# Score banks of an attention kernel as one tensor, with joint row maxima and one shift per group

## The reference

```
lat = layer_norm(layernorm(x));  c = layer_norm(ctx)        # with gains and biases
q = lat @ Wq;  k, v = split(concat([c, lat]) @ Wkv)         # 16 heads of 64; 487 keys
dots = q k^T / 8;  attn = softmax(dots);  out = (attn v) @ Wout
x = x + tanh(g_xattn) * out
x = x + tanh(g_ffn) * moe_ffn(layernorm(x))                 # 8 experts, top 2, gelu, width 1024
```

## Time and profile before

| | us |
|---|---|
| median of 3 runs | 1904.99 |
| lowest and highest run | 1902.63, 1905.17 |
| the profiled execution's own time | 1902.62 |
| span of its core in the trace | 1900.9 |
| first and last score maximum (line 495) start at | 74.7 and 1327.4 |
| busy TensorE / VectorE / ScalarE / GpSimd | 1674.2 / 1428.0 / 1195.3 / 1183.0 |

### The profile page before, as it was taken

One profiled execution on the slowest core, in us unless ns is written; L12 is line 12 of the kernel. 1 busy time (PEld: TensorE's weight loads), 2 busy tenths in 40 slices (PEclk: granted clock), 3 DMA queues, 4 the chain that ended last, 5 costly groups with the idle time before them and its releaser, 6 DMA issues. The chain is left out here.

```text
span 1900.9 us, 42714 instructions
## 1 busy us (share of the span) xinstructions
PE 1674.2 (88%) x15031; PEld 1163.1 (61%) x15032; DVE 1428.0 (75%) x2917; ACT 1195.3 (63%) x2666; POOL 1183.0 (62%) x1297
## 2 busy tenths in 40 slices
PE   2899999999999999999999999998402999999980
PEld 1456666666666666666666666665302999989970
DVE  4777888888888888888888888877395666666646
ACT  2587777777777777877777777777254333433320
POOL 4477777777777777777777777767263343333320
PEclk9999999999999999999999999999555999999995
DMA  3267766767767666676776776767455111111119
GB/s 131 46 127 140 142 144 131 139 139 142 147 129 145 138 140 144 135 139 138 139 150 136 136 137 129 138 130 142 118 186 173 46 49 45 50 50 47 47 35 289
DMA packets 599541, 233.18 MB, mean 123 GB/s; under 512 B 534064, under 2 KB 584016, under 8 KB 598992
## 3 DMA queue, kind: packets, MB, share of 16 engines
q1 hardware_dynamic: 592656, 212.67, 52.5%
q0 software_dynamic: 6720, 18.36, 3.1%
HBM read 78.66 MB, written 20.19 MB: 52 GB/s over the span
## 5 line engine op out<-in xcount | busy, mean ns | idle before, releaser
L279 POOL TENSOR_TENSOR p_parts<-p_f,p_parts 112x487 f16<-112x487 f32 x512 | 560.4, 1118 | 194.2 <-ACT p_parts L374 194.2
L365 ACT ACTIVATE p_f<-scores_ps,shift 112x487 f32<-112x487 f32 x512 | 337.0, 663 | 13.3 <-DVE shift L500 9.7
L495 DVE TENSOR_REDUCE neg_max<-scores_ps 112x1 f32<-112x487 f32 x512 | 313.0, 654 | 27.1 <-PE scores_ps L653 27.1
L402 ACT ACTIVATE k_hi<-proj_ps 128x488 fp32r<-128x488 f32 x256 | 147.9, 578 | 262.5 <-PE proj_ps L635 262.5
L1018 ACT ACTIVATE space<-h_ps,b_sb,undo 128x256 f32<-128x256 f32 x280 | 142.8, 560 | 232.1 <-PE h_ps L1247 228.8
L374 ACT ACTIVATE p_parts<-p_f 112x487 f16<-112x487 f32 x512 | 275.9, 607 | 0.0
L536 DVE SCALAR_TENSOR_TENSOR v_sb<-proj_ps,v_sb 128x512 f16<-128x512 f32 (+1 forms) x256 | 176.5, 689 | 92.1 <-ACT v_sb L416 89.4
L530 DVE TENSOR_TENSOR k_lo<-proj_ps,k_hi 128x488 fp32r<-128x488 f32 x256 | 168.2, 657 | 78.2 <-ACT k_hi L402 78.0
L684 PE MATMUL pv_ps<-v_sb,pt_sb 128*128 128x128 f16 x2048 | 218.9, 221 | 7.8 <-DMA pt_sb<-p_parts 7.8
L635 PE MATMUL proj_ps<-kv_hi,wkv_hi 128*128 128x488 f16 x512 | 192.3, 376 | 22.0 <-POOL kv_lo L306 13.5
L635 PE MATMUL proj_ps<-wkv_hi,kv_hi 128*128 128x512 f16 (+1 forms) x512 | 194.6, 380 | 0.1
(11 more groups left out here) (222 smaller groups left out, 4075.1 us busy)
## 6 DMA issues: line engine op xcount, KB each, us to landing
w_part<-in_L_ffn_w_dram SPq DMA_DIRECT2D x64, 256.0 KB, 3.5
stage<-in_L_ffn_w_dram SPq DMA_DIRECT2D x32, 512.0 KB, 4.1
ctx_sb<-in_ctx_dram SPq DMA_DIRECT2D x32, 375.0 KB
space<-y_rows SPq DMA_DIRECT2D x32, 224.0 KB, 4.7
pt_sb<-p_parts SPq DMA_TRANSPOSE x256, 4.0
x_sb<-in_x_dram SPq DMA_DIRECT2D x32, 112.0 KB
res_sb<-in_x_dram SPq DMA_DIRECT2D x32, 112.0 KB, 5.3
x_dram<-x_sb SPq DMA_DIRECT2D x32, 112.0 KB, 2.9
```

What stands on the lines that cost most here:

```text
L279: pool.tensor_tensor(p_parts[0:LQ, p % PS, h, 1, 0:LK], p_f[0:LQ, p % 2, h, 0:LK], p_parts[0:LQ, p % PS, h, 0, 0:LK], ALU.subtract).then_i ...
L365: act.activation(p_f[0:LQ, p % 2, h, 0:LK], scores_ps[n][0:LQ, 0:LK], ACT.Exp, bias=shift[0:LQ, p // 2 % 2, n:n + 1], accum_out=row_sum[0: ...
L402: act.activation(k_hi[:, j], ps[:, 0:LKP], ACT.Copy).then_inc(kq_high, 1)
L495: dve.tensor_reduce(neg_max[0:LQ, p // 2 % 2, n:n + 1], scores_ps[n][0:LQ, 0:LK], AX.X, ALU.max, negate=True).then_inc(max_done, 1)
```

## The change

The four score banks become one PSUM tensor of 128 by 4 by 512 numbers, with one bank for each value of the second index. VectorE takes the maxima of both heads of a pair by one instruction, which reads two banks, 112 by 2 by 487 numbers, and writes 2 numbers in each partition. It waits for both heads' scores. The shift is added by one instruction for the four heads of a group, after both maxima. ScalarE waits for it once in a group, ahead of the first exponential of the even pair; the odd pair no longer waits for a shift of its own. The order of all other instructions stays.

```
-        scores_ps = [bank(f"scores_ps{n}") for n in range(4)]
+        scores_ps = st.enter_context(nc.psum_tensor("scores_ps", [128, 4, 512], F32))
...
             def exponential(p, h):
                 if h == 0:
-                    act.wait_ge(bias_done, p + 1)
+                    if p % 2 == 0:
+                        act.wait_ge(bias_done, p // 2 + 1)
                     if p >= 2:
 
                         act.wait_ge(p_low, 2 * (p - 2) + 2)
                 n = 2 * (p % 2) + h
-                act.activation(p_f[0:LQ, p % 2, h, 0:LK], scores_ps[n][0:LQ, 0:LK], ACT.Exp, bias=shift[0:LQ, p // 2 % 2, n:n + 1],
+                act.activation(p_f[0:LQ, p % 2, h, 0:LK], scores_ps[0:LQ, n, 0:LK], ACT.Exp, bias=shift[0:LQ, p // 2 % 2, n:n + 1],
                                accum_out=row_sum[0:LQ, p // 2 % 4, n:n + 1]).then_inc(exp_done, 1)
...
-            def maximum(p, h):
-                n = 2 * (p % 2) + h
-                dve.wait_ge(scores_done, 2 * p + h + 1)
-                dve.tensor_reduce(neg_max[0:LQ, p // 2 % 2, n:n + 1], scores_ps[n][0:LQ, 0:LK], AX.X, ALU.max, negate=True).then_inc(max_done, 1)
+            def maximum(p):
+                n = 2 * (p % 2)
+                dve.wait_ge(scores_done, 2 * p + 2)
+                dve.tensor_reduce(neg_max[0:LQ, p // 2 % 2, n:n + 2], scores_ps[0:LQ, n:n + 2, 0:LK], AX.X, ALU.max, negate=True).then_inc(max_done, 1)
 
             def bias(p):
-                n = 2 * (p % 2)
-                dve.wait_ge(max_done, 2 * p + 2)
-                dve.tensor_scalar(shift[0:LQ, p // 2 % 2, n:n + 2], neg_max[0:LQ, p // 2 % 2, n:n + 2], P_SHIFT, None, ALU.add).then_inc(bias_done, 1)
+                dve.wait_ge(max_done, p + 2)
+                dve.tensor_scalar(shift[0:LQ, p // 2 % 2], neg_max[0:LQ, p // 2 % 2], P_SHIFT, None, ALU.add).then_inc(bias_done, 1)
...
                 if t % 2 == 0 and is_pair(t):
-                    maximum(t, 0)
-                    maximum(t, 1)
-                    maximum(t + 1, 0)
+                    maximum(t)
+                    maximum(t + 1)
                     bias(t)
-                    maximum(t + 1, 1)
-                    bias(t + 1)
```

More of the change, by code:

```diff
@@ L652, in _ @@
                                 rows = slice(64 * h, 64 * h + 64)
-                                last = nc.tensor.matmul(scores_ps[2 * (p % 2) + h][0:LQ, 0:LKP], qq[rows, p % NP], kk[rows, p % NP], start=(n == 0), stop=(n == 2))
+                                last = nc.tensor.matmul(scores_ps[0:LQ, 2 * (p % 2) + h, 0:LKP], qq[rows, p % NP], kk[rows, p % NP], start=(n == 0), stop=(n == 2))
                                 if n == 2:
```

## The result

The changed kernel takes 1980.87 us (median of 4 runs, 1978.07 to 1982.86); the kernel before, in the same comparison, 1904.08 us. The ratio is 1.0403, with a 95% interval from 1.0385 to 1.0421: the change makes the kernel 4% slower, by 77 us. The profiled execution took 1982.86 us, its span is 1981.1 us.

A forecast was written before the change was run, and what follows sets the result against it. TensorE was taken to pace the attention stage. Blocked shifts delay v_lo and k_lo, costing TensorE 2.1 us a batch, over 31 batches 66 us: 1969 from the profiled 1902.62, stated as 1971 us, range 1928 to 1992.

The forecast's parts named there:

- The maxima: VectorE: a joint maximum takes 1.16 us, saving 0.07 us a pair; waiting for both heads and bank names cost nothing.
- The shift: VectorE: the one shift, issued later, is blocked by GpSimd in all four groups, ending where the second ended before.
- j = 0: Group at j = 0: the V of j = 1 waits for the late v_lo, +0.18 us a batch.
- The rival that the time falls: k_lo starts sooner, so T and two K come sooner: 0.8 us a batch won, 1880 us; chance 0.08.
- The rival that half of the shifts escape: Half of the groups find GpSimd free, loss about 1 us a batch: 1936 us; chance 0.2.
- The rival that the shift isn't held: Shift not blocked, or delay hidden: -0.2 us a batch, no change told, 1900 to 1908 us; chance 0.05.
- j = 2: Group at j = 2: the K of j = 3 on TensorE starts later, +0.66 us a batch.
- The sum: TensorE's added waits over the four groups: 2.1 us a batch, 31 batches, 66 us.
- j = 4: Group at j = 4: the K of j = 5 on TensorE starts later, +0.81 us a batch.
- j = 6: Group at j = 6: V of j = 7 +0.17 us, and the Q behind the late k_lo +0.3 us, a batch.
- ScalarE's slack absorbs the delay before the next group: Attention stage: the delay does not pile up from batch to batch; ScalarE waits 162 us in 800 for TensorE.
- What I named as proof: Profile signs: maximum 1.16 us, shift median 0.5 or more, exponential waiting, K waits near 0.7 twice a batch, period 42.

The follow-up runs named there:

- run 3: The kernel before, with four single maxima in a row and then one shift for the group, no joint maximum, four banks as before: 1980.61 us, ratio 1.0409.
- run 5: The changed kernel's joint maxima, but a shift right behind each pair's maximum, and the maxima written to unused PSUM score-bank columns: 1880.26 us, ratio 0.9879.
- run 1: The changed kernel, same order and number of instructions, with the maxima written to unused PSUM score-bank columns so the one shift reads PSUM: 1905.02 us, ratio 1.0015.
- run 4: The changed kernel's joint maxima, but a shift for each pair right behind its maximum, maxima still in SBUF: 1976.22 us, ratio 1.0385.
- run 2: The kernel before, with only the maxima written to unused PSUM score-bank columns, so its two shifts a group read PSUM: 1882.26 us, ratio 0.9896.

## Why the prediction was right, point by point

**The bound.** Right: the attention stage is paced by TensorE, and everything that can be told is lost there, 76.4 us by the last maximum's start. The clock was costed at nothing, and the granted clock is 1.00 in every stretch from 400 to 1200 us, before and after.

**The maxima.** 1.16 us forecast from the rows of 487 and 1024 numbers, 1.162 measured. No cost of the joint read or of the names of banks: run 3 has the loss without them, run 5 has them without the loss.

**The shift.** Forecast: issued 2.27 us after the first maximum and held in all four groups, to end where the second one had ended. The group shown has 2.28 and 3.26 us. The forecast ends, at j = 0, 2, 4 and 6, were 2.96, 2.85, 3.27 and 3.34 us after the start of the first maximum; the medians of the trace are 2.97, 2.84, 3.26 and 3.30. (The prediction read the shifts' ends as about 0.05 us behind GpSimd's; taken one by one, the shifts of over 0.23 us end 0.02 to 0.03 us behind, before and after.) Runs 1 and 3 show both halves: it isn't held when its input is in PSUM, and a later issue doesn't change the end. The rule of the Trainium skill (SBUF — State Buffer, section Who interferes with whom) that I set beside the rows holds here for 4 numbers as for 2: 1018 ns at most in the changed kernel, and 160 to 163 with the input in PSUM. That GpSimd would wait in its turn for a shift issued first, no run here shows.

**The rival that the time falls** didn't come about. The advice of the Trainium skill beside it (VectorE: DVE Perf Modes, section Rules for kernel authors), to make chained operations fewer in count, did not pay here: 384 instructions fewer, and 77 us more.

**The rival that half of the shifts escape** didn't come about either: the exponential waited for the shift in 76 groups of 76.

**The rival that the shift isn't held** gave 1900 to 1908 us, and run 1 shows this case: 1905.02. That it lands within the range is in part luck. The gain of 0.2 us each at j = 0 and 6 is there, but j = 2 loses 0.50 us and not 0.24: its first maximum is late in run 1 too, a term that this sum, like the next, didn't have.

**The sum.** Here a term was too small. Forecast 2.1 us a batch, and 66 us in all. The last maximum came 76.4 us later, about 2.5 us a batch, and the period is 42.4. The distance on TensorE from the start of one group's scores to the next, as medians over 23 batches in the middle of the two traces, says where (the sum of the first column is the period before, 39.8 us):

| group | before | after | more | forecast |
|---|---|---|---|---|
| j = 0 | 8.47 | 8.69 | 0.22 | 0.18 |
| j = 2 | 10.16 | 11.14 | 0.99 | 0.66 |
| j = 4 | 11.80 | 12.63 | 0.83 | 0.81 |
| j = 6 | 9.43 | 9.90 | 0.48 | 0.17 + 0.3 |

Three of the four are right, and j = 2 is not. At j = 4: the K of j = 5 starts 815.02 - 809.70 = 5.32 us after the first maximum, before 811.96 - 807.46 = 4.50: 0.82, forecast 0.81. At j = 2 the forecast was 0.66. These are the scores and the K of j = 3 on TensorE after the change, and the group on VectorE:

```profile
797.18 0.48 PE L650 MATMUL scores_ps<-k_hi,q_hi 64*112 64x488 f32 x2
...
803.81 0.38 PE L632 MATMUL proj_ps<-kv_hi,wkv_hi 128*128 128x488 f16 x1 [0.74 <-DVE v_sb L533]
```

```profile
796.67 0.65 DVE L527 TENSOR_TENSOR k_lo<-proj_ps,k_hi 128x488 fp32r<-128x488 f32 x1
797.36 0.69 DVE L533 SCALAR_TENSOR_TENSOR v_sb<-proj_ps,v_sb 128x512 f16<-128x512 f32 x1
...
798.91 2.22 DVE L496 TENSOR_REDUCE neg_max<-scores_ps 112x2 f32<-112x974 f32 x2
801.17 0.59 DVE L500 TENSOR_SCALAR shift<-neg_max 112x4 f32<-112x4 f32 x1
```

and before the change the same scores, and the v_lo of j = 1, which stands ahead of the maxima of j = 2:

```profile
835.79 0.48 PE L653 MATMUL scores_ps<-k_hi,q_hi 64*112 64x488 f32 x2
```

```profile
835.65 0.69 DVE L536 SCALAR_TENSOR_TENSOR v_sb<-proj_ps,v_sb 128x512 f16<-128x512 f32 x1 [0.27 <-ACT v_sb L416]
```

From the scores to the K it was 841.43 - 835.79 = 5.64 us, it is 803.81 - 797.18 = 6.63: 0.99 more, and not 0.66. The missing 0.33 lies ahead of the shift. The first maximum started 837.20 - 835.79 = 1.41 us after the scores; now 798.91 - 797.18 = 1.73. What made it late is the v_lo of the group at j = 0, here after and then before:

```profile
789.87 2.24 DVE L496 TENSOR_REDUCE neg_max<-scores_ps 112x2 f32<-112x974 f32 x2
...
794.16 0.69 DVE L533 SCALAR_TENSOR_TENSOR v_sb<-proj_ps,v_sb 128x512 f16<-128x512 f32 x1 [0.74 <-ACT v_sb L417]
```

```profile
832.21 0.69 DVE L536 SCALAR_TENSOR_TENSOR v_sb<-proj_ps,v_sb 128x512 f16<-128x512 f32 x1
```

It starts 794.16 - 789.87 = 4.29 us after the start of its group's first maximum, before 832.21 - 828.70 = 3.51.

The step that failed is the sentence that "ScalarE's slack absorbs the delay before the next group, so it doesn't pile up from batch to batch". From batch to batch it doesn't. But between j = 0 and j = 2 neither ScalarE nor VectorE has that slack: VectorE stood idle there for 0.27 us only, ahead of that v_lo, and the v_lo of j = 0, 0.78 us later, pushes its list on. The group of j = 2 begins late against TensorE, and its shift is held on top of that. In run 1 that first maximum starts 1.66 us after the scores, with no shift held, so it is the lateness that pushes, whatever its cause. By 31 batches the 0.33 us are 10 us, nearly all of what the forecast loss of 66 us lacked against the 77 measured.

**What I named as proof** is there: the joint maximum at 1.16 us, the median of the shift above 0.5 (0.784), the wait of the exponential in each group, K waiting for v_lo twice a batch at 0.74 and 0.80, the period above 42.

## What to carry to other kernels

A tiny instruction on VectorE with input and output in SBUF can cost a whole instruction of GpSimd; its duration in the rows (minimum against median) shows that, and the time to look at is its end and not its length. Merging such instructions loses time if the one that is left stands behind more work and its consumer is the head of an in-order list: 25 us here (runs 1 and 5), with nothing held. The repair had two parts: a shift for each pair, close behind its maxima, and another home for the small operand (spare columns of a PSUM bank: 1880 to 1882 us) or another engine (1884). Each of these beats the kernel before by 1%. The other home alone, with the merged shift, gave 1905, no better than before.

## What the runs showed that I had not expected

The two ways of being late cost nearly the same by accident: in the changed kernel TensorE waits for v_lo, in run 4 for k_lo, and they differ by less than 5 us (1980.87 and 1976.22). Had only the times been compared, run 4 would have read as proof that joint maxima cost 74 us; run 5 shows that they cost nothing by themselves. The 1905 of run 1 is such an accident too: freeing the shift gains what the two shifts of before had lost by being held, 20 us, and the merged shift's later place takes it back. And freeing the shifts in the kernel before was worth 20 us, though the only visible wait there, 7.4 us in 800 for k_lo, comes to some 12 us over the stage: waits of TensorE that are shorter than the overlap of neighbouring matmuls don't stand in full in the list of waits. The K of j = 1 shows it: it starts 4.96 us after the scores of its group in the kernel before and 4.74 in run 2 (medians), while the trace of before shows 0.06 us of idle time ahead of it.
